# Graph kernel, one core: gathers without a bounds check, and the short last group of edges over 128 partitions

## The reference

```
edge_index_t = jnp.stack([src, dst], axis=1)
h = jnp.maximum(_layernorm(x, axis=-1), 0.0)
x = x + _L0_gnn_ref(h, ..., src, dst)            # layer 0
h = jnp.maximum(_layernorm(x, axis=-1), 0.0)
x = x + _L1_gnn_ref(h, edge_attr_32, edge_index_t, ...)   # layer 1

# layer 0
score = jnp.sum(feat[src] * feat[dst], axis=-1)
ez = jnp.exp(score - smax[dst])
a = ez / denom[dst]
msg = ft[src] * a[:, None]
agg = jax.ops.segment_sum(msg, dst, num_segments=N_NODES)
out = agg + jax.nn.relu(feat @ W_res + b_res)
out = (out - mean) * jax.lax.rsqrt(var + BN_EPS) * gamma + beta

# layer 1
msg_input = jnp.concatenate([node_i, node_j, edge_vectors], axis=1)   # rows of src and of dst
messages = _gelu(_gelu(msg_input @ W_m1 + b_m1) @ W_m2 + b_m2)
boxes = jax.ops.segment_sum(messages, edge_indices[:, 1], num_segments=...)
combined = _gelu(_gelu(concatenate([node_vectors, boxes]) @ W_c1 + b_c1) @ W_c2 + b_c2)
```

## Time and profile before

| what | value |
|---|---|
| median of 3 runs | 1828.24 us |
| lowest and highest run | 1814.08 and 1833.2 us |
| the profiled execution's own time | 1824.53 us |
| its span | 1822.7 us |
| busy: PE, DVE, ACT, POOL | 1313.4, 1351.0, 927.7, 1233.3 us |
| mean granted TensorE clock | 0.796 of full speed |

### The profile page before, as it was taken

How to read it: one execution, slowest core, us unless ns; L and a number is a source line. 1 busy time by engine, 2 the same in 40 slices (tenths; PEclk the granted TensorE clock), 3 DMA queues, 4 the chain that set the end, 5 groups by cost and what they waited for, 6 DMA issues and landing times.

```text
span 1822.7 us, 22166 instructions
## 1 busy us (share of the span) xinstructions
PE 1313.4 (72%) x6521; PEld 875.2 (48%) x6521; DVE 1351.0 (74%) x2253; ACT 927.7 (51%) x1840; POOL 1233.3 (68%) x1062
## 2 busy tenths in 40 slices
PE   3441756765737475275898898888885998899994
PEld 1231545554526354164666666566664443444431
DVE  7832776798649387187979998688854998799972
ACT  4511533453325242163666776476651776577772
POOL 7774664677765747500868887667867878887675
PEclk8755776786778676587888997798875999899996
DMA  7751764654435332125344554555555764566620
GB/s 216 258 177 34 285 231 155 209 200 141 117 95 166 100 114 90 36 99 220 110 160 157 194 185 161 163 176 189 174 160 127 183 162 121 133 146 156 139 49 16
DMA packets 132615, 273.56 MB, mean 150 GB/s; under 512 B 30404, under 2 KB 47658, under 8 KB 132496
## 3 DMA queue, kind: packets, MB, share of 16 engines
q1 hardware_dynamic: 76004, 187.38, 30.8%
q0 software_dynamic: 39360, 43.42, 12.0%
q10 hardware_dynamic: 17132, 41.35, 6.1%
HBM read 151.68 MB, written 121.80 MB: 150 GB/s over the span
## 4 chain that ended last, share of the span: by engine, by line
PE 29%; issue 24%; POOL 18%; another core or an unknown queue 10%; DVE 10%; ACT 5%; DMA 3%; ACTq 0%; SPq 0%; POOLq 0%; DVEq 0%
POOL agg_rows L609 11%; PE banks L1503 4%; POOL out L609 4%; PE banks L1387 3%; PE banks L1579 2%; DVE stat L772 2%; PE banks L1372 2%; PE banks L1577 2%; PE banks L1493 2%; PE banks L1586 2%; DVE stat L764 2%; PE banks L1553 2%; PE banks L1593 2%; POOL agg_ring L605 2%
## 5 line engine op out<-in xcount | busy, mean ns | idle before, releaser
L605 POOL DMA_INDIRECT part<-in_x,edge_idx x192 | 212.1, 1104 | 124.1 <-DVE part L774 66.3
L605 POOL DMA_INDIRECT agg_ring<-agg_rows,edge_idx x196 | 233.5, 1191 | 84.8 <-issue 56.4
L609 POOL DMA_INDIRECT agg_rows<-agg,put_first x196 | 232.2, 1185 | 58.0 <-issue 57.6
L609 POOL DMA_INDIRECT out<-agg,put_last x196 | 215.5, 1100 | 67.3 <-issue 59.8
L1503 PEld LDWEIGHTS banks<-packed,cT 97*128 97x128 f32 (+1 forms) x1568 | 216.3, 223 | 45.1 <-issue 45.1
L1372 PE MATMUL banks<-ident,xc 128*128 128x128 f32 (+1 forms) x784 | 137.6, 326 | 136.6 <-issue 76.4
L1503 PE MATMUL banks<-packed,cT 97*128 97x64 f32 (+1 forms) x1568 | 224.4, 309 | 0.0
L1099 ACT ACTIVATE hT<-banks 128x512 f32<-128x512 f32 (+1 forms) x98 | 55.5, 594 | 324.0 <-remote 165.4
L1387 PE MATMUL banks<-hT,packed 128*128 128x512 f32 (+1 forms) x196 | 132.2, 810 | 78.9 <-issue 54.3
L1372 PEld LDWEIGHTS banks<-ident,xc 128*128 128x128 f32 (+1 forms) x784 | 113.9, 177 | 147.5 <-issue 100.6
L1493 PE MATMUL banks<-hT,packed 64*96 64x512 f32 (+1 forms) x392 | 127.7, 730 | 59.6 <-ACT cT L1216 45.9
(11 more groups left out here) (166 smaller groups left out, 3195.2 us busy)
## 6 DMA issues: line engine op xcount, KB each, us to landing
xt<-in_x SPq DMA_DIRECT2D x84, 512.0 KB
r_rows<-rT ACTq DMA_DIRECT2D x48, 512.0 KB
agg_rows<-rb SPq DMA_DIRECT2D x48, 512.0 KB
out<-xt SPq DMA_DIRECT2D x36, 512.0 KB
edge_r<-rr ACTq DMA_DIRECT2D x48, 256.0 KB
rT<-r_rows SPq DMA_DIRECT2D x24, 512.0 KB
part<-r_rows SPq DMA_DIRECT2D x24, 512.0 KB
rr<-edge_r SPq DMA_DIRECT2D x48, 256.0 KB
```

What stands on the lines that cost most here:

```text
L605: A.indirect_dma_start(to, None, table[:, :], bass.IndirectOffsetOnAxis(ap=idx, axis=0), bounds_check=limit, oob_is_err=False).then_inc(si ...
L609: A.indirect_dma_start(table[:, :], bass.IndirectOffsetOnAxis(ap=idx, axis=0), rows_of, None, bounds_check=limit, oob_is_err=False).then_i ...
```

## The change

Gathers lose the two arguments of the bounds check; scatters keep them. The indirect DMAs of the short group, gathers and scatters, run over all 128 partitions; for the partitions 106 to 127 a gather reads row 0 of its table, and a scatter skips. What is done with the group otherwise stays at 106 partitions. The part of `agg` that belongs to the short group is set to zero by DVE at the very start, since the scatters now read 22 partitions of it that nothing writes.

```diff
             def gather(to, table, idx, signal):
-                A.indirect_dma_start(to, None, table[:, :], bass.IndirectOffsetOnAxis(ap=idx, axis=0),
-                                     bounds_check=limit, oob_is_err=False).then_inc(signal, 16)
+                A.indirect_dma_start(to, None, table[:, :], bass.IndirectOffsetOnAxis(ap=idx, axis=0)).then_inc(signal, 16)
...
             def gather_x(n):
                 g = group_of(n)
-                p = edges_of(g)
...
-                        gather(x_ring[n % GS][0:p, c:c + D], x, idx_of(idx, g, j, p), G_x.of(n))
+                        gather(x_ring[n % GS][:, c:c + D], x, idx_of(idx, g, j, P), G_x.of(n))
 
             def put_agg(n):
                 g = group_of(n)
-                p = edges_of(g)
...
-                    scatter(agg_rows, idx_of(put_first, g, j, p), agg_of(g, p)[:, j * D:(j + 1) * D], G_p.of(n))
+                    scatter(agg_rows, idx_of(put_first, g, j, P), agg_of(g, P)[:, j * D:(j + 1) * D], G_p.of(n))
 
             def gather_agg(g):
-                p = edges_of(g)
...
-                    gather(agg_ring[g % RS][0:p, j * D:(j + 1) * D], agg_rows, idx_of(src_idx, g, j, p), G_a.of(g))
+                    gather(agg_ring[g % RS][:, j * D:(j + 1) * D], agg_rows, idx_of(src_idx, g, j, P), G_a.of(g))
...
             def put_final(g):
-                p = edges_of(g)
...
-                    scatter(out, idx_of(put_last, g, j, p), agg_of(g, p)[:, j * D:(j + 1) * D], C_put.of(g))
+                    scatter(out, idx_of(put_last, g, j, P), agg_of(g, P)[:, j * D:(j + 1) * D], C_put.of(g))
...
+            V.memset(agg_of(G - 1, P), 0.0)
             V.memset(bias16[:, :, :], 0.0)
```

## The result

The changed kernel is slower. Its median is 1913.59 us (1899.32 to 1929.16, 4 runs) beside 1830.72 us for the kernel before (1814.08 to 1838.15, 4 runs): a ratio of 1.044 with a 95% interval of 1.0322 to 1.0557. The forecast was 1802 us, and its range ended at 1842. Medians here are of all runs of a kernel, while a ratio compares only the runs of each kernel that lie within 1.5% of its fastest, so the two can differ.

A forecast was written before the change was run, and what follows sets the result against it. No engine bounded the whole span; the first stage was DVE's 23 us rounds plus stalls ending when POOL ran dry. Terms 14.7 + 1.4 + 5.0 + 2.4 + 2.4 = 25.9 us took 1828.24 to 1802.3 us, range 1700 to 1842.

The forecast's parts named there:

- The price of the check: Cost of the bounds check per gather on POOL: taken as 0.04 us, between 0 and 0.34, pause left in place.
- the pause belongs to the check: Rival: the 0.30 us pause before POOL's gathers goes with the check, giving 1691 us; chance 0.13.
- The step that failed: First stage: stalls end when POOL runs dry, so 368 gathers of x save 0.04 us each, 14.7 us.
- c: The check's price per gather on POOL, taken as 0.04 us; values below 0 were excluded.
- The short group: 128 partitions instead of 106: 5.0 us from first gathers of x, 2.4 from scatters of agg, 2.4 from last scatters.
- The first wait for DVE: Sign in the first stage: POOL's first wait for DVE L774 would come near 156 us instead of 165.
- descriptors are free: Rival: generating the DMAs' descriptors shows no incremental cost, so nothing is gained, 1828 us; chance 0.04.
- The memset and the register instruction: DVE's added first memset and the register instruction removed before each gather group were both counted as costing nothing.
- Gathers of agg: Stage from 1107 us: 35 gathers on the chain save 1.4 us; the other 161 lie beside PE's work, nothing.
- More stalls, slower: Rival: denser gathers make PE's signals late in three more first-stage rounds, about 10 us each, 1848 us; chance 0.14.

The follow-up runs named there:

- the fastest kernel: The changed kernel with one 128x192 POOL memset after each gather of x, distance 1.38 us; 1716.2 us.

## Why the prediction was wrong

**The price of the check** was nearly right. I took 0.04 us; the gather went from 1.00 to 0.94 and the distance from 1.30 to 1.25, so it is 0.05 to 0.06, and the pause of 0.30 us stayed, as I had chosen. Rival *the pause belongs to the check* is out by that row.

**The step that failed** is the one that turned this price into time: "Each run of gathers ends in a POOL wait, and if stalls end there, all of c is on the path: 368 x 0.04 = 14.7 us." It was read from two stalls that ended behind POOL's last DMA. In the changed kernel a stall ends in the midst of POOL's stream (287.05 us, above), and a lead of four groups instead of eight moved the time by 23 to 34 us only. What the runs put in its place: while POOL issues indirect DMAs 1.25 to 1.33 us apart, PE's signals come late, and checked or not they come mostly on time at 1.38 us (1721 and 1716 us). The term has the other sign: 14.7 us were to be gained, and 76.8 us were lost in the first stage. Over the same 368 gathers that is 0.21 us lost for each one that became some 0.05 us shorter. I had kept c at or above zero because nothing is added to a gather; that is true of the gather's own time and says nothing about what its rate does to others.

**The short group.** Durations came as predicted: first gathers 0.94 us, last scatters 0.97 instead of 1.56. The first wait for DVE did not come near 156 us but at 108.64, with the chain of waits on late signals since 57 us (11.15 us at 87.56), so DVE was already late by then. From DVE's last instruction to the end of POOL's last scatter it is 1877.97 to 1891.97 = 14.0 us; before it was 14.7. Of the 2.4 us at the end 0.7 arrived: the queue of scatters behind DVE's last instruction was longer. By itself the part makes no difference that can be measured (1.0108 [0.985, 1.0365]). The rival *descriptors are free* has the duration wrong for this DMA, whose 128 rows take less time than 106; its time for this part, no gain, can't be told from what was measured.

**The memset and the register instruction** cost nothing, as said: DVE now waits 1.13 us for the first rows of x instead of 1.86, and the run with the wait on the first gather is at 1.0008. **Gathers of agg**: 1.4 us were predicted from 1107 us on, and the second stage is 2.4 us shorter; too little to tell from chance.

**The rival "More stalls, slower"** named what the runs showed, that denser gathers make signals late in more rounds, and three things in it were off. I gave it three rounds, and it took nearly the whole stage. I priced a new stall at 10 us; the pieces of the chain above have 13 to 22. And I let stalls end only when POOL runs dry. Its 1848 us was 66 us short of the result, and its chance of 0.14 was too low. The evidence was in the trace: PE's signals were late where POOL issued without a break, and that speaks of POOL's pace. I should have asked what a denser pace does before asking how much sooner it ends.

What stays open is the mechanism in the chip. The runs show that the pace of indirect DMAs on POOL changes how late PE's signals are, that breaks of 2.3 us help and that more distance within the stream helps. They don't show where a signal of PE is held. Nor is it shown why 0.05 us more, from 1.33 to 1.38 us, brings 134 us (1850 to 1716), when 1.30 and 1.33 lie together.

## What to carry to other kernels

When an engine waits long for a signal although its producer is done, look at what a third engine issues at that moment, and vary its rate in both directions before trusting that less work there is a gain. Here 0.05 us less per gather cost 4.4%. A useless memset that put 0.13 us between the gathers then gave the changed kernel 10% (1914 to 1716 us). The same trick on the checked kernel made it 5.1% faster than the one before. A stream of DMAs that is dense and far ahead of need is a candidate for pacing. A wait for the landing of the group before is the simplest form of it and needs no idle instruction, but it gained less (1791 us). The best distance tried was 1.38 us. At 1.44, which is the round divided by its gathers (23 us / 16), POOL was already the bound (1765 us): some gathers take longer than the bare one, so aim below that quotient.

## What the runs showed of the hardware

- PE's signals came late, in single waits by up to 54 us, while POOL issued indirect DMAs at distances of 1.25 to 1.33 us, and far less often at 1.38 us and more: the waits of ACT's copy for them fell from 254.7 us (25 of them) in the changed kernel to 62.5 us (3) in the fastest. The one of 49.2 us that is left stands beside scatters, 1.28 us apart.
- Late signals come with idle and with busy DMA engines: their share is 0.08 in the 23 us window above, and 0.62 from 275 to 287 us of the changed kernel, in the stall that ends at 287.05.
- The pause in front of an indirect DMA on POOL depends on what stands ahead of it: 0.30 us behind another indirect DMA, 0.16 behind a memset of 128x128 to 128x256, 0.19 behind one of a single column. A memset of 128x192 (0.28 us) therefore moves the next gather by only 0.13 us (1.38 instead of 1.25).
- A gather beside busy engines can take over twice its time, checked or not (up to 2.39 us in the checked kernel with a distance of 1.38, 2.80 us in the unchecked one), so a mean of a group says little about the bare price.
- A wait for the landing of eight gathers cost POOL mostly 2.2 to 2.7 us, sometimes 6.
- The granted TensorE clock rose with the stalls gone: 0.77 of full speed in the first stage of the fastest kernel beside 0.71 before, and PE's busy time there fell from 478 to 453 us for the same instructions.
